# Attention and routed experts on one core: two heads stacked for one output product, a reworked passage between the two phases, and the combining of the experts' rows in 37 single steps

## What is computed

```python
x  = L0_attn_x                     # (4, 1024, 128) float32
xn = layernorm(x)
# causal attention, 16 heads of 64
n  = xn / max(norm(xn), 1e-12) * sqrt(128) * gamma
q, k, v = split_heads(n @ w_qkv)
a  = softmax(where(causal, (q * 64**-0.5) @ k.T, -big)) @ v
attn = concat_heads(a) @ w_out     # (1024 -> 128)
# 8 experts, the best 2 for each token
logits = xn @ Wr.T + br; top 2, softmax over them
o   = sum over the two experts of weight * (relu(xn @ W1[e].T + b1[e]) @ W2[e].T + b2[e])
ffn = layernorm(xn + o) * ffn_gamma + ffn_beta
out = x + attn + ffn
```

## Time and profile before

| what | value |
|---|---|
| time, median of 3 runs | 1564.49 us (1564.24 to 1565.29) |
| profiled execution | 1564.66 us, span 1562.8 us |
| granted TensorE clock over the span | 0.969 |
| PE busy | 1449.6 us (93%) |
| DVE busy | 1076.4 us (69%) |
| ACT busy | 1067.4 us (68%) |
| POOL busy | 907.1 us (58%) |
| output product L1350 | 155.9 us busy, 1024 records |

### The profile page before, as it was taken

One profiled execution on the slowest core, in us unless ns is written; L12 is line 12 of the kernel. 1 busy time (PEld: TensorE's weight loads), 2 busy tenths in 40 slices (PEclk: granted clock), 3 DMA queues, 4 the chain that ended last, 5 costly groups with the idle time before them and its releaser, 6 DMA issues.

```text
span 1562.8 us, 28739 instructions
## 1 busy us (share of the span) xinstructions
PE 1449.6 (93%) x9130; PEld 1126.8 (72%) x9131; DVE 1076.4 (69%) x2341; ACT 1067.4 (68%) x2590; POOL 907.1 (58%) x923
## 2 busy tenths in 40 slices
PE   3559999699999999999999999999999999999998
PEld 3548888467777777777777777777777777777776
DVE  6565555457776877687768776876687668866883
ACT  2445566267777777777777777777777777777775
POOL 0762000157666766676667666766676667666766
PEclk9579999689999999999999999999999999999999
DMA  9122211111111111111111111111111111111111
GB/s 311 46 79 71 58 54 52 44 35 42 33 28 38 40 33 29 38 40 33 29 38 40 33 28 40 38 33 28 39 38 33 28 41 37 33 28 42 37 28 55
DMA packets 58759, 72.34 MB, mean 46 GB/s; under 512 B 7400, under 2 KB 44560, under 8 KB 58640
## 3 DMA queue, kind: packets, MB, share of 16 engines
q1 hardware_dynamic: 40720, 52.57, 14.2%
q10 hardware_dynamic: 13824, 9.86, 2.0%
q0 software_dynamic: 4096, 8.40, 1.8%
HBM read 20.47 MB, written 16.52 MB: 24 GB/s over the span
## 4 chain that ended last, share of the span: by engine, by line
PE 66%; DVE 9%; ACT 3%; issue 2%; DMA 1%; SPq 0%; POOLq 0%; POOL 0%; DVEq 0%; ACTq 0%
PE max_ps L1291 9%; PE score_ps L1316 8%; PE score_ps L1317 8%; PE misc_ps L1350 8%; PE head_ps L1333 7%; PE head_ps L1337 7%; PE head_ps L1335 7%; PE misc_ps L1267 3%; DVE q_a L1125 3%; PE max_ps L1294 2%; PE score_ps L1319 2%; DVE row_max L1135 2%; ACT p_hi L1082 1%; PE misc_ps L1261 1%; PE misc_ps L1300 1%
## 5 line engine op out<-in xcount | busy, mean ns | idle before, releaser
L1033 POOL TENSOR_TENSOR p_lo<-probs,p_hi 128x512 fp32r<-128x512 f32 (+3 forms) x768 | 775.0, 1025 | 415.1 <-ACT p_hi L1082 408.7
L1082 ACT ACTIVATE probs<-score_ps 128x512 f32<-128x512 f32 (+3 forms) x768 | 375.4, 489 | 236.2 <-PE score_ps L1319 168.6
L1135 DVE TENSOR_REDUCE row_max<-max_ps 128x1 f32<-128x128 f32 (+7 forms) x512 | 386.7, 756 | 157.2 <-PE max_ps L1294 146.7
L1082 ACT ACTIVATE p_hi<-score_ps 128x512 fp32r<-128x512 f32 (+3 forms) x768 | 373.2, 486 | 0.0
L1333 PE MATMUL head_ps<-p_hi,v_hi 128*65 128x512 f32 (+3 forms) x768 | 295.2, 384 | 0.3 <-POOL p_lo L1033 0.3
L1316 PE MATMUL score_ps<-q_a,k_a 128*128 128x512 f32 (+3 forms) x768 | 266.6, 347 | 3.1 <-DMA q_b<-shift 3.1
L1317 PE MATMUL score_ps<-q_b,k_b 65*128 65x512 f32 (+3 forms) x768 | 266.9, 348 | 0.0
L1291 PE MATMUL max_ps<-k_a,q_a 128*128 128x384 f32 (+5 forms) x768 | 249.6, 380 | 16.4 <-DVE row_max L1135 12.6
L1337 PE MATMUL head_ps<-p_lo,v_hi 128*65 128x512 f32 (+3 forms) x768 | 258.7, 337 | 0.0
L1335 PE MATMUL head_ps<-p_hi,v_lo 128*64 128x512 f32 (+3 forms) x768 | 258.5, 337 | 0.0
L1316 PEld LDWEIGHTS score_ps<-q_a,k_a 128*128 128x128 f32 x768 | 144.8, 189 | 46.4 <-issue 3.7
(11 more groups left out here) (170 smaller groups left out, 2106.0 us busy)
## 6 DMA issues: line engine op xcount, KB each, us to landing
k_a<-k_a SPq DMA_DIRECT2D x64, 256.0 KB, 3.3
q_b<-q_a SPq DMA_DIRECT2D x64, 256.0 KB, 4.2
sorted_x<-zeros SPq DMA_DIRECT2D x13, 384.0 KB, 15.2
w_raw<-sorted_x SPq DMA_DIRECT2D x26, 192.0 KB, 2.5
sorted_y<-result ACTq DMA_DIRECT2D x78, 64.0 KB, 1.6
acc<-in_L_attn_x_dram SPq DMA_DIRECT2D x4, 512.0 KB, 9.0
w_raw<-in_L_ffn_W_dram ACTq DMA_DIRECT2D x1, 2048.0 KB, 22.7
q_b<-shift SPq DMA_DIRECT2D x128, 2.0 KB
```

The lines of the kernel that those rows point to most:

```text
L1033: pool.tensor_tensor(p_lo[:, slot, 0:w], probs[:, slot, 0:w], p_hi[:, slot, 0:w].bitcast(F32), ALU.subtract).then_inc(p_split, 1)
L1082: ins = act.activation(p[:, (g * CH + c) % RING, 0:width], score_ps[(g * CH + c) % 2][:, 0:width], ACT.Exp, scale=SCALE)
L1135: dve.tensor_reduce(row_max[:, g % 2, t:t + 1], src, axes, ALU.max).then_inc(max_taken, 1)
```

## The change

**Output product.** The two heads of a pair are stacked in `heads` (128 rows) and multiplied by a full 128 x 128 piece of the weights, once per pair: two units (`Y_AT`) of four tiles, at chunk 8 of the next even head and chunk 4 of the odd head behind it. So the denominators must be applied before. ACT copies each finished half to `raw`; then a chain (`CHAIN`) follows, per head and half: SP folds the denominator row into 16 partitions (`den`), DVE inverts it (`inv`), SP stores it to DRAM, SP reads it back spread over 64 partitions (`scale`), and DVE multiplies `raw` by `scale` into `heads` (`normalise`, at chunks 3 and 7). TensorE's `y` waits for `normalised`. `add_y` is one DVE instruction for four tiles. `probs` has 4 buffers in place of 6, and ACT waits for `p_split` four chunks back.

**Passage.** The weights of the first block are split in the first phase (`w_hi`, `w_lo`). ACT no longer waits for the last stores; SP and POOL do, before they use `sorted_y`. Before the first scores only the four narrow maximum parts run; the wide ones of head 0 stand beside its chunks 0 to 2, and the parts for head 1 at chunks 3 to 10.

**Combining.** 37 steps, one instruction each (`moments` has four), at eight chunks of heads 3 to 7 of the block. The `gsc` copies are gone.

```diff
@@ the walk
-            COMBINE_AT = [(g, c) for g in (3, 4, 5) for c in (0, 2, 3, 6, 7, 10, 11)][:10 + RSQRT_STEPS]
-            COMBINE_STEPS = 11 + RSQRT_STEPS
-            Y_AT = [6, 9, 10]
-            y_units = [(0, 3), (3, 3), (6, 2)]
+            COMBINE_STEPS = len(COMBINE)
+            COMBINE_AT = [(g, c) for g in (3, 4, 5, 6, 7) for c in (0, 1, 2, 3, 5, 7, 9, 11)][:COMBINE_STEPS]
+            Y_AT = {8: 0, CH + 4: 1}
+            CHAIN = [("fold", 5), ("invert", 8), ("store", 9), ("spread", 12), ("normalise", 16)]
+            FIRST_WIDE = {0: (4, 5), 1: (6,), 2: (7,)}
+            FIRST_MAX_AT = [3, 4, 5, 6, 7, 8, 9, 10]
...
+                for kind, lag in CHAIN:
+                    if at >= lag and (at - lag) // CH < ALL_HEADS and (at - lag) % CH in LAST:
+                        order.append((kind, (at - lag) // CH, LAST.index((at - lag) % CH)))
@@ SP
+                    def fold_denominator(g, half):
+                        sp.wait_ge(raw_out, n_half(g, half) + 1)
+                        sp.dma_start(den[:, half], raw[HEAD:HEAD + 1, g % 2, half].rearrange("o (f n) -> o f n", f=FOLD)
...
+                    def store_inverse(g, half):
+                        sp.wait_ge(inverted, n_half(g, half) + 1)
...
+                    def spread_inverse(g, half):
+                        sp.wait_ge(inv_stored[half], 16 * g + 16)
@@ ACT
-                                act.wait_ge(pv_done, n_chunk(hp, g, c) + 1)
-                                for p in (probs, p_hi):
+                            act.wait_ge(pv_done, n_chunk(g, c) + 1)
+                            if n_chunk(g, c) >= PROBS:
+                                act.wait_ge(p_split, n_chunk(g, c) - PROBS + 1)
...
+                            if g >= 2:
+                                act.wait_ge(normalised, n_half(g - 2, half) + 1)
+                            act.activation(raw[:, g % 2, half], head_ps[0:HEAD + 1, cols],
+                                           ACT.Copy).then_inc(raw_out, 1)
@@ DVE
+                    def invert(g, half):
+                        dve.wait_ge(den_folded[half], 16 * g + 16)
+                        dve.reciprocal(inv[:, half], den[:, half]).then_inc(inverted, 1)
+                    def normalise(g, half):
+                        dve.wait_ge(scale_spread[half], 16 * g + 16)
+                        dve.tensor_tensor(heads[s * HEAD:(s + 1) * HEAD, cols], raw[0:HEAD, s, half], scale[:, half],
+                                          ALU.mult).then_inc(normalised, 1)
+                        dve.tensor_tensor(acc[:, toks], misc_ps[u % 2][:].rearrange("p (t d) -> p t d", t=GROUP),
+                                          acc[:, toks], ALU.add).then_inc(y_added, 1)
@@ PE
+                    def project_out(p, n, u):
+                        pe.wait_ge(normalised, n_half(2 * p + 1, n) + 1)
...
+                            ins = pe.matmul(dst[:, t * D:(t + 1) * D], heads[:, q0:q0 + P], wo[:],
+                                            start=True, stop=True)
```

More of the change, by code:

```diff
@@ L917, in n_chunk @@
[L917 to L937 removed]
+            order = [(kind, 0, n) for n in range(6) for kind in ("project", "project_lo")]
```

555 lines of the change are left out of this document (261 added, 294 removed).

## The result

The changed kernel takes 1568.6 us (median of 11 runs, 1567.16 to 1570.62), the kernel before on the same chips 1564.61 us (1563.82 to 1565.44). The ratio is 1.0025 (95% interval 1.0016 to 1.0034). I forecast 1558 and faster; it is slower, by just over what such a measurement can tell. The range held the time. (The combining has 36 steps in the code, not the 37 of the title: four each of centre, first, second, stats and scale, eleven of the inverse root, and five single ones.)

The account below looks back on a forecast made before the run. It took TensorE, with VectorE only 0.3 us from being late in even heads, to bound the kernel. Blocks -7, passage -5 and end +5.5 gave -6.5 us on 1564.66, about 1558 us; range 1515 to 1583.

Parts of the forecast that it names:

- the blocks: Attention's eight blocks of eight heads: 154.5 us each against 155.4, so -7 us in all.
- the passage: From the last stores to attention's first chunks: earlier start -2.4 us, earlier scores -3, together -5; bounds -2.4 and -10.
- the end: From ScalarE's last copy to the last addition: about 10 us against 4.5, so +5.5; bounds +4 and +9.
- What bounds the kernel: In attention's even heads VectorE is nearly as late as TensorE; a 0.3 us margin at m6 decides the change.
- The unit held at chunk 8: Even head: TensorE's output product waits for the second `normalise`, losing 1.44 us of the 1.98 freed per pair of heads.
- the first interval: Chunk-1 transposition of a block's head 0 to that of head 2, without combining: 37.6 us, plus small odd-head waits.
- N: Duration of VectorE's `normalise`: 0.7 to 0.85 us at chunk 3, 1.0 at chunk 7; bounds 0.68 and 1.67.
- The interval 2 to 4: Head 2's transposition to head 4's: 37.9 us with `normalise` at 1.0 us beside the gathers, plus odd-head waits.
- Combining in even heads: Steps in heads 4 and 6 delay VectorE's maxima and `normalise`: intervals of 38.9 and 38.4 us, before odd-head waits.
- The last interval: Head 6's transposition to the next block's: 38.4 us from short combining steps, plus waits in head 7.
- The order of the maxima: Before the first scores, wide maximum parts moved beside chunks 0 to 2: chunk 4 at 321.5 against 324.95, taken as -3.
- Rival 3: Slower, `normalise` held up as a rule: at 1.16 us everywhere 157.1 us per block, about 1578 us; chance 0.22.

Follow-up runs that it names:

- run 1: Changed kernel with the even head's output product unit at chunk 11 in place of chunk 8; 1558.79 us.
- run 4: Changed kernel without GpSimd's subtraction, TensorE taking the high part of the probabilities in place of the low; 1522.25 us.
- run 14: Changed kernel with units at chunks 11 and 9, gathers spread and combining steps in odd heads 3, 5 and 7; 1524.08 us.
- run 2: Changed kernel without the combining steps on VectorE, gathers kept and waited for but not used; 1541.07 us.
- run 7: Changed kernel with combining begun four slots later, at chunk 5 of head 3 in place of chunk 0; 1566.02 us.
- run 11: Changed kernel with GpSimd's eight gathers spread over chunk 4 of head 0 to chunk 3 of head 2; 1557.51 us.
- run 9: Changed kernel with the old order of the maximum parts before the first scores; 1566.18 us.
- Run 10: Changed kernel without the three DMAs of each half, so the output isn't divided by the denominators; 1567.20 us.
- run 12: Changed kernel with the combining steps alone moved, one at each chunk of heads 3, 5 and 7; 1582.95 us.
- run 13: Changed kernel with combining steps in odd heads and units at chunks 11 and 9, gathers still bunched; 1540.18 us.
- run 8: Changed kernel with combining steps in groups of four, at the kernel before's chunks in heads 3 to 5; 1649.58 us.

## Why the prediction was wrong

**By terms.** The sum was -7 for the blocks, -5 for the passage and +5.5 for the end. Between the two profiled executions the pairs behind the first gave +1.8, the passage with the first pair -1.5, the end +6.2, and the stretch ahead of it -0.4. The blocks' term is the one that was furthest off, by 9 us; without that miss the kernel would have come out faster.

**What bounds the kernel: right.** VectorE's lateness decides. TensorE's 29 us of saved busy time didn't shorten the span, and runs 1, 4 and 14 win time by making VectorE less late or by asking for its result later, not by making TensorE faster.

**The unit held at chunk 8: right, with both of its terms too large.** I had 37.6 to 37.7 us for the first interval; it is 37.72, and run 1 shows that the place of the unit costs. But the profile shows 0.49 us of idle time at the unit where I had 1.44. And the output product freed less than 1.98 us: counted from the start of each of its products to the start of the next, waits left out, the traces give 3.41 us per pair of heads before and 1.77 after, so 1.64. The rest of the loss is in small waits, most of them at the maximum parts and below what the profile names. That the interval came out right is in part luck.

**N: right in its mean, wrong in its worst case.** I took 0.7 to 1.0 us; it is 0.85. I had bounded a held-up instruction by 1.67, on the ground that "the wait is only the rest of one subtraction". This is the step that failed: the first centre step was held up beside three subtractions, 3.47 us. The four centre steps stand in head 3, and I had 0.3 us for all the waits of that head, because VectorE has slack in odd heads. The gathers of head 2 I had at another 0.3. The interval 2 to 4 was forecast at 38.2 and measured at 39.74. Run 2 divides the difference: the combining steps cost 1.2 us in it (39.74 against 38.51), the gathers 0.8 without any step (38.51 against 37.71). Runs 7 and 11 show that it needn't be: there it is 38.8 and 38.1.

**Combining in even heads: undersized a little.** Forecast 39.1 for 4 to 6, measured 39.82. The steps cost 1.7 us there where I had 1.5; the interval is 38.14 without them, not 37.6, and in run 2's trace TensorE waits 0.35 us in it for VectorE's split of the next block's weights, which I had left out. The last interval I oversized, by 1.3. Over a block combining costs 3.4 us (27.5 / 8) against 2.7 before, and this 0.8 eats the 0.9 us per block that I forecast as gain.

**The passage: -5 forecast, wrong in kind.** The earlier start gave 1.4 us (first product 285.91), not 2.4. The order of the maxima, for which I took -3, costs about 3: I had counted products and waits, and not the granted clock, which the windows of run 9 point to. In the traces the first chunk of half 1 did start at 321.08, as forecast (321.5); what was lost came behind it. The trace of the kernel before had shown the clock's place too, 0.50 in the four microseconds ahead of this window and 1.00 behind it, and I didn't look:

```profile
320.00:324.00 4.00, 3.89 (x17) 2.53 (x17) 3.47 (x6) 3.31 (x9) 0.62 (x3) 0.69 0.01 2
```

**The end: +5.5 forecast, +6.2 measured**, with the spread at 3.04 us in place of 2.3 to 2.7. Run 10 shows that it is the DMA chain.

**Rival 3** had the sign and a mechanism near the truth, but `normalise` at 1.16 throughout is not what happened; its mean is 0.85, and a few long hold-ups, the gathers and the steps together did it.

## What to carry to other kernels

Work taken off the busiest engine is a gain only where that engine isn't waiting for the one that gets new work; read the margin at the handover first, and place new steps behind it. An instruction that another engine can hold up may wait through more than one of that engine's instructions: look for the stretches in which that engine runs without a gap and price what stands there apart. Here it was worth more to break up such a stretch (eight gathers moved, 11 us) than to move the steps out of it (under 3 us). When the pieces of a change interact, try them together: here a move that costs 14 us alone is part of a version 47 us faster than the changed kernel, and 2.7% faster than the one before.

## What the hardware showed that I had not expected

A VectorE instruction that reads and writes SBUF was held up beside more than one GpSimd instruction. The centre step takes 0.34 us without the subtractions (run 4), 3.47 us in the run of ten subtractions, 3.44 in a run of eight (run 12), where a subtraction takes at most 1.31; two `normalise` of run 13 take 2.25 and 2.52 us, against 0.67 in run 4. The Trainium skill ("SBUF — State Buffer", Who interferes with whom) says that VectorE and GpSimd share a port pair under an exclusive lock, that a VectorE instruction contends for it in a 2-port perf mode, or with two SBUF inputs against a GpSimd instruction that reads SBUF, and that in the first case the second to issue is blocked until the other's whole instruction is done. In which mode the centre step ran, no trace shows. By that rule the wait would end with the subtraction under way, at 1.3 us or less. The trace agrees that the step is held up and disagrees on the length; the measurement decides. That the lock isn't passed on between instructions without a gap is my reading and was not tried by itself.

TensorE's granted clock fell to 0.50 around an idle stretch of 4.0 us (run 8), and stayed there for about 5 us of full work. At the start of attention in the changed kernel it went from 0.90 back to 0.53 (windows at run 9) with waits of 1.6 and 0.8 us, while the waits of up to 1.3 us within its blocks left it at 1.00.
